# Conv attention with softmax over 256 keys: values of two row pairs in four column quarters, row sums from key tiles that GpSimd adds, and one turn of the context per eight rows

## Chip, cores and metric

One core of one Trainium2 chip runs the whole kernel as one launch. The metric is the device time of that core in microseconds; lower is better. The kernel before takes 2170.26 us, the median of 3 runs.

## The reference

A batch of 16 images with 128 channels and 32 x 32 pixels goes through three layers. The change touches the first alone:

```
g = group norm of x                                        # 32 groups of 4 channels
q = einsum('bchw,oc->bohw', g, qW)                         # 256 outputs: 8 heads x 32
k = einsum(..., BN(depthwise 3x3, stride 2, of g), kW)     # 32 x 256 keys
v = einsum(..., BN(depthwise 3x3, stride 2, of g), vW)     # 256 values x 32
attn = softmax(q.k / sqrt(4), over the 256 keys)           # q reshaped to rows of 32
ctx = attn @ v;   x = x + einsum('bchw,oc->bohw', ctx, oW)
```

Causal attention over each image's 1024 tokens and a mixture of 8 experts follow.

## The kernel before

The program has three blocks with a barrier between them: `conv_attention`, then `attention_and_routing`, then `expert_tiles`. Each engine's work is an instruction queue of its own, written out by hand, and semaphores are the only ties between them.

In `conv_attention` the work on an image is a period of eight turns, one for each pair (`i` from 0 to 7). A pair stands for four rows `h` of the queries, each with 256 columns of them, so 1024 softmax rows. `over_images` runs the periods as a loop over two images with the first and last written out. The stages of one pair are spread over several turns:

- `scores` (TensorE) makes plain scores of the pair `i + 3` in two banks `s_bank`, a row at a time; `row_max` (VectorE) reduces each to the negated maximum over keys.
- `turn_maxes` transposes the maxima of pair `i + 2` into `m_bank`; `max_high` (ScalarE) and `max_low` (VectorE) split them; SyncE's `shift_rows` sends them as two rows below the queries in `q_stack`.
- `shifted_scores` of pair `i` come out transposed, keys on partitions, in two banks `st_bank`, in two chunks `c` of 512 columns; `exps` (ScalarE) takes the exponential into `probsT`.
- `values` of pair `i - 1`: the stationary tile `v_ones` has 32 columns of values, one of ones for the row sums, and zeros up to 64. The two chunks go to the two column halves of the array and so to the two halves of the partitions of `o_bank`.
- `evacuate_context` (ScalarE) copies `o_bank` to `ctxT`; in the next turn `turn_context` transposes it into `c_bank`, and `normalise` (VectorE) takes the reciprocal of the sums there and multiplies.

Beside that run, for a coming image: `channel_stats`, `group_means`, `group_spread`, `group_variances`, `group_norm`, then `keys_values` (nine taps, each a matmul, whose stationary tile holds three copies of the key weights and one of the values' in 128 columns) and `queries` in four parts. `query_high`, `query_low` split each part, and SyncE (`queries_in`, eight transfers) and GpSimd (`queries_low_in`, four) lay it out in `q_stack`. `project` and `add_output` make the result of half an image. All of these use one bank, `front`.

What orders the work around the change is the text of each engine's `period`. On TensorE a turn reads so before, and this is the order that the times below belong to:

```
shifted_scores(b, slot, i, 0); turn_context(pair i - 2)
scores(pair i + 3, 0); scores(.., 1); turn_maxes(pair i + 2)
shifted_scores(b, slot, i, 1)
[group_variances at i == 0, group_means at i == 7]
values(pair i - 1)
scores(pair i + 3, 2); scores(.., 3)
[keys_values at 1; queries at 0, 2, 4, 6; project at 3 and 7]
```

## Time and profile before

| | us |
|---|---|
| median of 3 runs (2168.64 to 2171.3) | 2170.26 |
| the profiled execution, its own time | 2174.15 |
| its span, first to last instruction | 2172.4 |
| TensorE busy in the span | 1961.4 |
| VectorE busy | 1375.0 |
| ScalarE busy | 989.7 |
| GpSimd busy | 1029.3 |

The span is what the trace covers; the profiled execution's time has 1.75 us around it. Busy time is an average over three blocks that have different limits. The conv attention runs from the start to about 841 us; its last projection starts at 839.66 us and the next block's first scores at 842.84 us. In the rows, L733 are the shifted scores, L715 the scores, L745 the values, L753 the turned context, L723 the turned maxima, L635 the taps, L657 the queries, L678 the projection. A matmul of 32-bit floats with a plain (not the rounded, `F32R`) type shows as two records.

### The profile page before, as it was taken

The numbers are of one execution on the slowest core, as the hardware profiler recorded it, in microseconds if no ns is written. First come the engines' busy times: TensorE is split into PE (matmuls) and PEld (weight loads), VectorE is DVE, ScalarE is ACT, GpSimd is POOL, SyncE is SP. The second block draws the span as 40 slices with busy tenths as digits, with TensorE's granted clock in tenths as the row PEclk, the third lists the DMA queues.
The fourth block names the chain that finished last, engine by engine and source line by source line (L and its number), as shares of the span: only waits on it lengthen the run. The fifth ranks groups of instructions, "written<-read, shape, count | busy, mean of one in ns | idle before, by whom it ended". The sixth has DMA issues, their size and how long they took to land. (4 is left out here: it accounts for less than half of the span.)

```text
span 2172.4 us, 44335 instructions
## 1 busy us (share of the span) xinstructions
PE 1961.4 (90%) x11636; PEld 1466.1 (67%) x11636; DVE 1375.0 (63%) x3923; ACT 989.7 (46%) x2194; POOL 1029.3 (47%) x1367
## 2 busy tenths in 40 slices
PE   3999999999999998888898888887189999999997
PEld 2666666666666654665666666555189999999997
DVE  3676766767767665787788878876434444444443
ACT  0554555555455554444344333342045555555554
POOL 1221121212112111445554555555658888888887
PEclk9999999999999999999999999998589999999999
DMA  5322222222223222111111111111234444454454
GB/s 195 74 66 71 61 71 64 65 70 65 70 60 73 62 61 74 54 36 38 41 38 41 36 38 35 42 38 40 66 57 64 64 65 63 63 65 65 63 65 51
DMA packets 175423, 131.90 MB, mean 61 GB/s; under 512 B 33437, under 2 KB 164933, under 8 KB 175301
## 3 DMA queue, kind: packets, MB, share of 16 engines
q0 software_dynamic: 55808, 52.50, 15.1%
q1 hardware_dynamic: 118341, 77.16, 13.6%
q8 instruction: 86, 1.41, 0.3%
q10 hardware_dynamic: 1152, 0.54, 0.1%
q14 instruction: 36, 0.29, 0.0%
HBM read 31.47 MB, written 46.71 MB: 36 GB/s over the span
## 5 line engine op out<-in xcount | busy, mean ns | idle before, releaser
L1664 POOL DMA_INDIRECT out<-f_y,f_rows x272 | 424.1, 1559 | 45.5 <-POOL f_waited L1662 41.7
L447 DVE TENSOR_REDUCE neg_max<-s_bank 128x2 f32<-128x512 f32 x512 | 329.5, 685 | 133.5 <-PE s_bank L715 131.4
L1727 DVE SCALAR_TENSOR_TENSOR f_hidden<-f_silu,f_rows,f_h_bank 128x341 f32<-128x341 f32 x272 | 155.4, 571 | 307.6 <-ACT f_silu L1696 279.7
L567 ACT ACTIVATE probsT<-st_bank 128x512 f32<-128x512 f32 x512 | 276.6, 593 | 133.9 <-PE st_bank L733 133.6
L1096 POOL DMA_INDIRECT routed<-a_rows,a_target_idx x256 | 253.2, 989 | 68.6 <-issue 68.3
L335 POOL TENSOR_TENSOR waited<-nothing 128x1 int32<-128x1 int32 x64 | 12.1, 189 | 514.0 <-DVE q_low L436 514.0
L1473 PE MATMUL a_score_bank<-t_eT,t_gT 128*128 128x512 f32 x512 | 252.4, 617 | 1.2 <-DVE a_val L1140 1.2
L745 PE MATMUL o_bank<-probsT,v_ones 128*64 128x512 f32 x1024 | 248.0, 605 | 0.0
L1775 PE MATMUL f_y_bank<-w,f_hiddenT 114*128 (+1 forms) x1632 | 230.8, 277 | 1.3 <-ACT f_hiddenT L1688 1.3
L715 PEld LDWEIGHTS s_bank<-k_stack,q_stack 96*128 96x128 f32 x1024 | 141.9, 193 | 113.4 <-issue 94.0
L733 PE MATMUL st_bank<-q_stack,k_stack 98*128 98x512 f32 x512 | 214.0, 484 | 0.6 <-ACT probsT L567 0.5
L1775 PEld LDWEIGHTS f_y_bank<-w,f_hiddenT 114*128 114x128 f32 (+1 forms) x1632 | 203.1, 191 | 8.5 <-issue 1.8
L715 PE MATMUL s_bank<-k_stack,q_stack 96*128 96x256 f32 x1024 | 195.9, 312 | 6.9 <-DMA q_stack<-q_high 6.0
L1498 PE MATMUL a_sum_bank<-a_val,a_causal_probsT 128*128 128x129 f32 x1152 | 162.7, 289 | 41.1 <-DVE X L1204 36.9
L1688 ACT ACTIVATE f_hiddenT<-f_hT_bank 114x384 f32<-114x384 f32 x272 | 133.8, 492 | 144.2 <-issue 74.6
L1756 PE MATMUL f_h_bank<-w_high,f_xT_high 128*128 x544 | 196.3, 363 | 0.0
L1498 PEld LDWEIGHTS a_sum_bank<-a_val,a_causal_probsT 128*128 128x128 f32 x1152 | 147.7, 201 | 67.0 <-issue 61.0
L1696 ACT ACTIVATE f_silu<-f_h_bank 128x341 f32<-128x341 f32 x272 | 124.2, 457 | 124.1 <-PE f_h_bank L1759 122.3
L1185 DVE TENSOR_REDUCE a_row_neg_max<-a_score_bank 128x1 f32<-128x1024 f32 x128 | 155.8, 1217 | 37.3 <-PE a_score_bank L1473 19.7
L1106 POOL TENSOR_TENSOR a_causal_probs<-a_causal_probs,a_tril 128x128 f32<-128x128 f32 x128 | 58.5, 457 | 252.9 <-DVE a_causal_probs L1192 246.0
L1756 PE MATMUL f_h_bank<-w,f_xT_high 128*128 x544 | 173.1, 320 | 0.0
L1369 ACT ACTIVATE a_causal_probs<-a_score_bank,a_row_neg_max 128x128 f32<-128x128 f32 (+7 forms) x128 | 94.7, 740 | 141.0 <-DVE a_row_neg_max L1185 141.0
(210 smaller groups left out, 3591.7 us busy)
## 6 DMA issues: line engine op xcount, KB each, us to landing
q_stack<-q_high SPq DMA_DIRECT2D x512, 64.0 KB, 2.3
f_rows<-routed SPq DMA_DIRECT2D x272, 66.0 KB
q_stack<-q_low POOLq DMA_DIRECT2D x256, 64.0 KB, 2.6
out<-X SPq DMA_DIRECT2D x16, 512.0 KB, 3.2
X<-in_x SPq DMA_DIRECT2D x1, 6144.0 KB, 22.1
out<-f_y,f_rows POOLq DMA_INDIRECT x272
q_stack<-max_rows SPq DMA_DIRECT2D x256, 4.0 KB
routed<-a_rows,a_target_idx POOLq DMA_INDIRECT x256
```

The source lines that it names most:

```text
L447: dve.tensor_reduce(neg_max[:, i % 2, CT * j:CT * (j + 1)], s_bank[h % 2][:], AX_X, ALU.max, negate=True).then_inc(max_ready, 1)
L567: act.activation(probsT[:, i % 2, c, lt, :], st_bank[lt][:], ACT.Exp).then_inc(exp_done, 1)
L715: last = pe.matmul(s_bank[h % 2][:, t, :], q_stack[0:STACK, h, t * P:(t + 1) * P], k_stack[0:STACK, slot, :], start=(t == 0), stop=(t == C ...
L733: pe.matmul(st_bank[lt][:], k_stack[:, slot, lt * P:(lt + 1) * P], q_stack[:, h:h + 2, :].rearrange("p h c -> p (h c)"), start=True, stop= ...
L745: last = pe.matmul(o_bank[HALF * c:HALF * (c + 1), :], v_ones[:, slot, lt, :], probsT[:, i % 2, c, lt, :], start=(lt == 0), stop=(lt == LT ...
L1096: pool.indirect_dma_start(out=routed, out_offset=bass.IndirectOffsetOnAxis(ap=target_idx[:, slot, t, k:k + 1], axis=0), in_=rows[:, slot, ...
L1185: dve.tensor_reduce(neg_max[:, i % 2:i % 2 + 1], s_bank[i % 2][:], AX_X, ALU.max, negate=True).then_inc(max_ready, 1)
L1473: last = pe.matmul(s_bank[i % 2][:, 512 * h:512 * (h + 1)], gT[:, slot, i * P:(i + 1) * P], eT[:, slot, 512 * h:512 * (h + 1)], start=True ...
L1498: last = pe.matmul(o_bank[:], probsT[:, i % 2, t, :], val[:, slot, t, :], start=(t == 0), stop=(t == i))
L1664: pool.indirect_dma_start(out=out, out_offset=bass.IndirectOffsetOnAxis(ap=rows[:, i, TOKEN:TOKEN + 1].bitcast(I32), axis=0), in_=y[:, i, ...
L1756: pe.matmul(bank[:, 0:PADDED], xT_high[:, n % (2 * AHEAD), :], parts[part][:, of_expert], start=(part == 0), stop=False, skip_group_check= ...
L1775: last = pe.matmul(y_bank[:], hiddenT[0:m, n % 2, j, :], w2[0:m, bass.ds(e, 1), j, :], start=(j == 0), stop=(j == CHUNKS - 1))
```

## The change

Pairs are taken two by two, as octets of eight rows. `values` runs for an octet, in even turns, after `scores` of rows 2 and 3: the four chunks go to the four column quarters (`QUAD` = 32), with stationary tiles of 32 columns of values and no ones. The row sums come apart from that: GpSimd adds the two key tiles of each chunk (`add_keys`, into free halves of `tokens.eT` and `tokens.gT`) and four matmuls with the selector `ones_at` write the sums of octet `o` to row `o` of each quarter of a new bank, `sum_bank`. `m_bank` is given up for it: the turned maxima now go to the first quarter of `c_bank`. The context is turned once per octet, in odd turns, and ScalarE copies it unscaled to `raw` (`evacuate_turned`). The sums of an image are turned, inverted and applied in turns 2 and 3 of the next image (`turn_sums`, `invert_sums`, `scale`), and the two projections move to turns 3 and 5 there. The nine taps are split in five and four, with 64-column tiles in the two column halves; VectorE adds the halves (`keys_values`), and `split_keys` makes its copies from the one set of keys. `q_high` and `q_low` have two slots, and `probsT` has four.

```diff
+        v_rows = sb("v_rows", [P, 2, LT, KD])
+        ones_at = sb("ones_at", [P, OCTETS, QUAD])
+        q_high = sb("q_high", [P, Q_SLOTS, 2, CP], F32R)
+        q_low = sb("q_low", [P, Q_SLOTS, 2, CP], F32R)
...
-        probsT = sb("probsT", [P, 2, CHUNKS_PER_PAIR, LT, COLS])
+        probsT = sb("probsT", [P, 4, CHUNKS_PER_PAIR, LT, COLS])
         ctxT = sb("ctxT", [P, 2, COLS])
-        rsum = sb("rsum", [P, 2, 4, 2])
-        context = sb("context", [P, ROWS, CT, KD])
+        sumT = sb("sumT", [P, COLS])
+        rsum = sb("rsum", [P, ROWS * CT])
+        raw = sb("raw", [P, ROWS * CT, KD])
+        context = sb("context", [P, ROWS * CT, KD])
...
-        m_bank = ps("m_bank", [P, P])
+        sum_bank = ps("sum_bank", [P, COLS])
+        m_bank = c_bank[:, 0, :]
+        def key_sum(cc):
+            return (tokens.eT, tokens.gT)[cc // 2][:, 1, COLS * (cc % 2):COLS * (cc % 2 + 1)]
...
+                def add_keys(b, i):
+                    if i % 2 == 0:
+                        wait(pool, o_full, octet_no(b, i // 2))
+                    for c in range(CHUNKS_PER_PAIR):
+                        pool.wait_ge(exp_done, PAIR_EXPS * pair_no(b, i) + LT * (c + 1))
+                        pool.tensor_tensor(key_sum(CHUNKS_PER_PAIR * (i % 2) + c), probsT[:, i % 4, c, 0, :],
+                                           probsT[:, i % 4, c, 1, :], ALU.add).then_inc(key_sums, 1)
...
                 def keys_values(b, slot):
                     dve.wait_ge(kv_full, b + 1)
-                    dve.tensor_scalar(kv[:, slot, :], front[:, 0:L], kv_bias[:], None, ALU.add).then_inc(kv_ready, 1)
+                    dve.tensor_scalar(kv[:, slot, :], front[KV:2 * KV, 0:L], kv_bias[:], None, ALU.add
+                                      ).then_inc(kv_half, 1)
+                    dve.wait_ge(kv_half, b + 1)
+                    dve.tensor_tensor(kv[:, slot, :], kv[:, slot, :], front[0:KV, 0:L], ALU.add).then_inc(kv_ready, 1)
...
-                def normalise(b, slot, i):
...
-                                      .to_broadcast([P, 2, 4, KD]), ALU.mult).then_inc(ctx_done, 1)
...
+                def invert_sums(b):
+                    dve.wait_ge(sums_turned, b + 1)
+                    dve.reciprocal(rsum[:].rearrange("p (j c n) -> p j c n", j=OCTETS, c=OCTET_CHUNKS),
+                                   c_bank[:].rearrange("p n (c j) -> p j c n", j=QUAD)[:, 0:OCTETS]
+                                   ).then_inc(rsum_ready, 1)
+                    dve.wait_ge(rsum_ready, b + 1)
+                def scale(b, k):
+                    dve.wait_ge(c_out, OCTETS * (b + 1))
+                    wait(dve, out_full, 2 * (b - 1) + k + 1)
+                    part = slice(ROWS * k, ROWS * (k + 1))
+                    dve.tensor_tensor(context[:, part, :], raw[:, part, :],
+                                      rsum[:, part].unsqueeze(2).to_broadcast([P, ROWS, KD]), ALU.mult
+                                      ).then_inc(scaled, 1)
...
-                        turned = pair(b, slot, i - 2)
-                        if has(turned[0]):
-                            normalise(*turned)
+                        if i == 2 and has(b - 1):
+                            invert_sums(b - 1)
                         turning = pair(b, slot, i + LEAD - 1)
                         if has(turning[0]):
                             max_low(*turning)
+                        if i == 2 and has(b - 1):
+                            scale(b - 1, 0)
...
+                            scale(b - 1, 1)
+                            add_output(b - 1, 0)
...
+                def evacuate_context(b, slot, o):
+                    act.wait_ge(o_full, octet_no(b, o) + 1)
+                    wait(act, c_full, octet_no(b, o) - 1)
+                    act.activation(ctxT[:, o % 2, :], o_bank[:], ACT.Copy).then_inc(ctxT_full, 1)
+                    if o == OCTETS - 1:
+                        act.activation(sumT[:], sum_bank[:], ACT.Copy).then_inc(sums_out, 1)
+                def evacuate_turned(b, slot, o):
+                    act.wait_ge(c_full, octet_no(b, o) + 1)
+                    wait(act, scaled, 2 * b - (o < OCTETS // 2))
+                    rows = slice(2 * PAIR_ROWS * CT * o, 2 * PAIR_ROWS * CT * (o + 1))
+                    act.activation(raw[:, rows, :].rearrange("p (c n) d -> p n c d", c=OCTET_CHUNKS),
+                                   c_bank[:].rearrange("p n (c d) -> p n c d", d=KD), ACT.Copy).then_inc(c_out, 1)
...
+                    halves = ((4, 0, 1, 2, 7), (5, 3, 6, 8))
+                    for n in range(len(halves[0])):
+                        for part, taps in enumerate(halves):
+                            if n == len(taps):
+                                continue
+                            t = taps[n]
+                            di, dj = divmod(t, 3)
+                            out = front[KV * part:KV * (part + 1), 0:L].rearrange("p (i j) -> p i j", j=SIDE // 2)
+                            last = pe.matmul(out[:, di == 0:, dj == 0:], tap_w[:, t, :],
+                                             xn[:, (1, 0, 1)[di]:SIDE - (di == 0):2, (1, 0, 1)[dj]:SIDE - (dj == 0):2],
+                                             start=(n == 0), stop=(n == len(taps) - 1), skip_group_check=True)
...
-                def values(b, slot, i):
-                    if i == 0:
+                def values(b, slot, o):
+                    if o == 0:
                         pe.wait_ge(v_in, 16 * LT * (b + 1))
-                    pe.wait_ge(exp_done, PAIR_EXPS * (pair_no(b, i) + 1))
-                    wait(pe, ctxT_full, pair_no(b, i))
+                        wait(pe, sums_out, b)
+                    pe.wait_ge(key_sums, OCTET_CHUNKS * (octet_no(b, o) + 1))
+                    wait(pe, ctxT_full, octet_no(b, o))
                     for lt in range(LT):
-                        for c in range(CHUNKS_PER_PAIR):
-                            last = pe.matmul(o_bank[HALF * c:HALF * (c + 1), :], v_ones[:, slot, lt, :],
-                                             probsT[:, i % 2, c, lt, :], start=(lt == 0), stop=(lt == LT - 1))
+                        for cc in range(OCTET_CHUNKS):
+                            i, c = divmod(cc, CHUNKS_PER_PAIR)
+                            pe.matmul(o_bank[QUAD * cc:QUAD * (cc + 1), :], v_rows[:, slot, lt, :],
+                                      probsT[:, (2 * o + i) % 4, c, lt, :], start=(lt == 0), stop=(lt == LT - 1))
+                    for cc in range(OCTET_CHUNKS):
+                        last = pe.matmul(sum_bank[QUAD * cc:QUAD * (cc + 1), :], ones_at[:, o, :], key_sum(cc),
+                                         start=(o == 0), stop=(o == OCTETS - 1), skip_group_check=True)
                     last.then_inc(o_full, 1)
-                def turn_context(b, slot, i):
-                    pe.wait_ge(ctxT_full, pair_no(b, i) + 1)
-                    wait(pe, ctx_done, pair_no(b, i))
+                def c_bank_free(b, i):
+                    turning = pair(b, 0, i + LEAD - 1)
+                    wait(pe, m_low_done, pair_no(turning[0], turning[2]) if has(turning[0]) else PAIRS * NB)
+                def turn_context(b, slot, o):
+                    pe.wait_ge(ctxT_full, octet_no(b, o) + 1)
+                    wait(pe, c_out, octet_no(b, o))
+                    wait(pe, rsum_ready, b)
                     for n in range(4):
-                        last = pe.transpose(c_bank[:, n, :], ctxT[:, i % 2, n * P:(n + 1) * P], ident[:])
+                        last = pe.transpose(c_bank[:, n, :], ctxT[:, o % 2, n * P:(n + 1) * P], ident[:])
                     last.then_inc(c_full, 1)
+                def turn_sums(b):
+                    pe.wait_ge(sums_out, b + 1)
+                    pe.wait_ge(c_out, OCTETS * (b + 1))
+                    for n in range(4):
+                        last = pe.transpose(c_bank[:, n, :], sumT[:, n * P:(n + 1) * P], ident[:])
+                    last.then_inc(sums_turned, 1)
...
+                        summed = octet(b, slot, i)
+                        turned = i % 2 and has(summed[0])
+                        if turned:
+                            c_bank_free(b, i)
+                            turn_context(*summed)
+                        if i == 2 and has(b - 1):
+                            c_bank_free(b, i)
+                            turn_sums(b - 1)
                         if has(scored[0]):
                             scores(*scored, 0)
                             scores(*scored, 1)
                         if has(turning[0]):
+                            if turned:
+                                pe.wait_ge(c_out, octet_no(summed[0], summed[2]) + 1)
+                            if i == 2:
+                                wait(pe, rsum_ready, b)
                             turn_maxes(*turning)
                         if has(b):
                             shifted_scores(b, slot, i, 1)
@@ -773,12 +847,11 @@
                             group_variances(new)
                         if i == PAIRS - 1 and has(b + 2):
                             group_means(b + 2)
-                        summed = pair(b, slot, i - 1)
-                        if has(summed[0]):
-                            values(*summed)
                         if has(scored[0]):
                             scores(*scored, 2)
                             scores(*scored, 3)
+                        if i % 2 == 0 and has(summed[0]):
+                            values(*summed)
...
                         if i == 3 and has(b - 1):
+                            project(b - 1, 0)
+                        if i == 5 and has(b - 1):
                             project(b - 1, 1)
-                        if i == PAIRS - 1 and has(b):
```

TensorE in two neighbouring turns. Before, one turn from turning the context to scores of rows 2 and 3; `x3` are repeats:

```order
L753 MATMUL c_bank<-ident,ctxT 128x128 [waits ctx_done,ctxT_full]
L753 MATMUL c_bank<-ident,ctxT 128x128 x3
L715 MATMUL s_bank<-k_stack,q_stack 128x256 [waits max_ready]
L715 MATMUL s_bank<-k_stack,q_stack 128x256
L715 MATMUL s_bank<-k_stack,q_stack 128x256 [waits max_ready]
L715 MATMUL s_bank<-k_stack,q_stack 128x256
L723 MATMUL m_bank<-ident,neg_max 128x128 [waits m_low_done,max_ready]
L733 MATMUL st_bank<-q_stack,k_stack 128x512 [waits exp_done] x2
L745 MATMUL o_bank<-probsT,v_ones 64x512 [waits ctxT_full,exp_done]
L745 MATMUL o_bank<-probsT,v_ones 64x512 x3
L715 MATMUL s_bank<-k_stack,q_stack 128x256 [waits max_ready]
L715 MATMUL s_bank<-k_stack,q_stack 128x256
```

In the changed kernel an odd turn, from turning the context of an octet:

```order
L811 MATMUL c_bank<-ident,ctxT 128x128 [waits c_out,rsum_ready,ctxT_full,m_low_done]
L811 MATMUL c_bank<-ident,ctxT 128x128 x3
L761 MATMUL s_bank<-k_stack,q_stack 128x256 [waits q_low_in0,max_ready,q_in0,k_ready]
L761 MATMUL s_bank<-k_stack,q_stack 128x256
L761 MATMUL s_bank<-k_stack,q_stack 128x256 [waits max_ready]
L761 MATMUL s_bank<-k_stack,q_stack 128x256
L769 MATMUL c_bank<-ident,neg_max 128x128 [waits m_low_done,max_ready,c_out]
L779 MATMUL st_bank<-q_stack,k_stack 128x512 [waits exp_done] x2
L761 MATMUL s_bank<-k_stack,q_stack 128x256 [waits max_ready]
L761 MATMUL s_bank<-k_stack,q_stack 128x256
L761 MATMUL s_bank<-k_stack,q_stack 128x256 [waits max_ready]
L761 MATMUL s_bank<-k_stack,q_stack 128x256
```

and the end of the even turn before it, from the scores of row 3 to the queries:

```order
L761 MATMUL s_bank<-k_stack,q_stack 128x256 [waits max_ready]
L761 MATMUL s_bank<-k_stack,q_stack 128x256
L793 MATMUL o_bank<-probsT,v_rows 32x512 [waits ctxT_full,key_sums]
L793 MATMUL o_bank<-probsT,v_rows 32x512 x7
L796 MATMUL sum_bank<-t_eT,ones_at 32x512 x2
L796 MATMUL sum_bank<-t_gT,ones_at 32x512 x2
L709 MATMUL front<-qwT,xn 128x256 [waits out_done,q_low_done]
L709 MATMUL front<-qwT,xn 128x256
```

The values no longer stand between the two pairs of scores, and the turned maxima of an odd turn wait for `c_out`, which `evacuate_turned` raises.

ScalarE in the changed kernel, an odd turn and the even one after it: L609 are the exponentials, L623 is the copy of the turned context, L602 the maxima, L614 the copy of `o_bank`, L595 the queries:

```order
L609 ACTIVATE probsT<-st_bank 128x512 [waits st_full,o_full]
L609 ACTIVATE probsT<-st_bank 128x512 [waits st_full]
L623 ACTIVATE raw<-c_bank 128x4x4x32 [waits scaled,c_full]
L602 ACTIVATE max_rows<-c_bank 8x128 [waits m_in1,m_full]
L609 ACTIVATE probsT<-st_bank 128x512 [waits st_full] x2
L609 ACTIVATE probsT<-st_bank 128x512 [waits st_full,o_full]
L609 ACTIVATE probsT<-st_bank 128x512 [waits st_full]
L602 ACTIVATE max_rows<-c_bank 8x128 [waits m_in0,m_full]
L609 ACTIVATE probsT<-st_bank 128x512 [waits st_full] x2
L614 ACTIVATE ctxT<-o_bank 128x512 [waits c_full,o_full]
L595 ACTIVATE q_high<-front 128x512 [waits q_in3,q_full]
```

Before, the odd turn had no instruction between its exponentials and the maxima, and `ctxT` was copied in every turn:

```order
L567 ACTIVATE probsT<-st_bank 128x512 [waits st_full,o_full]
L567 ACTIVATE probsT<-st_bank 128x512 [waits st_full]
L560 ACTIVATE max_rows<-m_bank 8x128 [waits m_in1,m_full]
L567 ACTIVATE probsT<-st_bank 128x512 [waits st_full] x2
L572 ACTIVATE ctxT<-o_bank 128x512 [waits c_full,o_full]
```

VectorE in turns 1 and 2, where keys and values arrive. Before:

```order
L422 TENSOR_SCALAR kv<-front,kv_bias 128x256 [waits kv_full]
L426 CAST k_stack<-kv 64x256 [waits kv_ready]
L427 CAST k_high<-kv 32x256
L429 TENSOR_TENSOR k_stack<-kv,k_high 32x256 [waits k_high_ready]
L447 TENSOR_REDUCE neg_max<-s_bank 128x2 [waits m_full,s_full]
L447 TENSOR_REDUCE neg_max<-s_bank 128x2 [waits s_full]
L465 RECIPROCAL rsum<-c_bank 128x2x4 [waits c_full,out_done]
```

and in the changed kernel:

```order
L459 TENSOR_SCALAR kv<-front,kv_bias 64x256 [waits kv_full]
L462 TENSOR_TENSOR kv<-kv,front 64x256 [waits kv_half]
L466 CAST k_stack<-kv 32x256 [waits kv_ready]
L467 CAST k_stack<-kv 32x256
L469 TENSOR_TENSOR k_stack<-kv,k_stack 32x256 [waits k_high_ready]
L487 TENSOR_REDUCE neg_max<-s_bank 128x2 [waits m_full,s_full]
L487 TENSOR_REDUCE neg_max<-s_bank 128x2 [waits s_full]
L500 RECIPROCAL rsum<-c_bank 128x64 [waits sums_turned]
L493 TENSOR_TENSOR max_rows<-c_bank,max_rows 8x128 [waits m_high_done,rsum_ready]
```

There is one more operation before the keys are split, and between the row maxima and `max_low` stands a reciprocal of 64 elements, for whose end the turned maxima wait.

## Rows read from the trace of the kernel before

**Rows 1.** The page: the span, and busy time, share and instructions by engine.
```profile
span 2172.4 us, 44335 instructions
...
PE 1961.4 (90%) x11636; PEld 1466.1 (67%) x11636; DVE 1375.0 (63%) x3923; ACT 989.7 (46%) x2194; POOL 1029.3 (47%) x1367
```

**Rows 2.** One image by windows: length, busy of PE, PEld, DVE, ACT, POOL; clock.
```profile
401.20:450.30 49.10, 48.37 (x247) 30.14 (x246) 34.25 (x75) 25.29 (x53) 10.12 (x21) 1.00 0.27 66
```

**Rows 3.** Timeline of TensorE: the shifted scores that open turns 1 to 0, and 1.
```profile
404.55 0.81 PE L733 MATMUL st_bank<-q_stack,k_stack 98*128 98x512 f32 x2
...
413.09 0.82 PE L733 MATMUL st_bank<-q_stack,k_stack 98*128 98x512 f32 x2
...
418.44 0.83 PE L733 MATMUL st_bank<-q_stack,k_stack 98*128 98x512 f32 x2
...
424.74 1.02 PE L733 MATMUL st_bank<-q_stack,k_stack 98*128 98x512 f32 x2
...
430.31 0.82 PE L733 MATMUL st_bank<-q_stack,k_stack 98*128 98x512 f32 x2
...
435.20 0.64 PE L733 MATMUL st_bank<-q_stack,k_stack 98*128 98x512 f32 x2
...
440.66 0.82 PE L733 MATMUL st_bank<-q_stack,k_stack 98*128 98x512 f32 x2
...
447.97 1.03 PE L733 MATMUL st_bank<-q_stack,k_stack 98*128 98x512 f32 x2
...
453.66 0.82 PE L733 MATMUL st_bank<-q_stack,k_stack 98*128 98x512 f32 x2
```

**Rows 4.** Timeline of turn 5: start, length, engine, line, operation, count.
```profile
430.70 0.60 ACT L553 ACTIVATE q_high<-front 128x512 fp32r<-128x512 f32 x1 [0.93 <-PE front L657]
...
430.97 0.60 PE L753 MATMUL c_bank<-ident,ctxT 128*128 128x128 f32 x4
431.19 1.08 ACT L567 ACTIVATE probsT<-st_bank 128x512 f32<-128x512 f32 x2
...
431.88 0.27 PE L723 MATMUL m_bank<-ident,neg_max 128*128 128x128 f32 x1
...
431.91 0.91 PE L733 MATMUL st_bank<-q_stack,k_stack 98*128 98x512 f32 x2
...
432.75 1.94 PE L745 MATMUL o_bank<-probsT,v_ones 128*64 128x512 f32 x8
...
434.62 0.74 PE L715 MATMUL s_bank<-k_stack,q_stack 96*128 96x256 f32 x4
```

**Rows 5.** Timeline of TensorE at the first records of a group of values.
```profile
432.75 0.65 PE L745 MATMUL o_bank<-probsT,v_ones 128*64 128x512 f32 x2
```

**Rows 6.** Timeline of TensorE: taps, a projection, a part of the queries.
```profile
409.44 4.01 PE L635 MATMUL front<-xn,tap_w 128*128 128x256 f32 x18
...
423.42 1.88 PE L678 MATMUL front<-context,owT 128*128 128x512 f32 x4
...
429.63 1.03 PE L657 MATMUL front<-qwT,xn 128*128 128x256 f32 x4
```

**Rows 7.** Timeline of VectorE in turn 7.
```profile
443.81 1.29 DVE L447 TENSOR_REDUCE neg_max<-s_bank 128x2 f32<-128x512 f32 x2
```

**Rows 8.** Timeline of VectorE after the taps: keys, then the first row maxima.
```profile
413.48 0.48 DVE L422 TENSOR_SCALAR kv<-front,kv_bias 128x256 f32<-128x256 f32 x1 [2.80 <-PE front L635]
...
415.06 1.29 DVE L447 TENSOR_REDUCE neg_max<-s_bank 128x2 f32<-128x512 f32 x2
```

**Rows 9.** GpSimd's groups by form: busy, mean ns of one, idle before.
```profile
L337 POOL DMA_DIRECT2D q_stack<-q_low x256 | 143.7, 567 | 2.9 <-issue 2.9
...
L1106 POOL TENSOR_TENSOR a_causal_probs<-a_causal_probs,a_tril 128x128 f32<-128x128 f32 x128 | 58.5, 457 | 252.9 <-DVE a_causal_probs L1192 246.0 <-issue 6.2
...
L1091 POOL TENSOR_TENSOR w<-w,w_high 128x341 fp32r<-128x341 f32 x16 | 14.2, 910 | 6.1 <-ACT w_high L1390 6.1
```

**Rows 10.** VectorE's output sum, 300 to 600 us, by form.
```profile
L476 DVE TENSOR_TENSOR X<-X,front 128x512 f32 x13 | 8.9, 688 | 9.8 <-PE front L678 9.8
```

155 lines of the change are left out of this document (66 added, 89 removed).

## The prediction

> **What bounds the kernel now.** I read the page first [rows 1]: TensorE is busy for 90% of the span, but over three stages with different limits, and the change touches only the first, the conv attention of 16 images. The view by windows and the timeline of the shifted-score matmuls, which open every turn of the loop over row pairs, give that stage's rhythm [rows 2, 3]. The reader is to see eight turns per image, of 4.9 to 8.5 us, 49.1 us together, 16 times; in them TensorE 48.4 us busy, VectorE 34.3, ScalarE 25.3, GpSimd 10.1. So TensorE's queue sets the pace. But its busy time holds waits: in turn 5 [rows 4] the second pair of shifted scores takes 0.91 us where the same pair in turn 6 takes 0.64 at 435.20, pipeline included [rows 3], because its bank waits for an exponential. What the array must stream is, for a turn, 0.86 for two shifted pairs, 0.44 to turn the context (four records in 0.60, 0.17 of it pipeline [rows 4]), 0.96 for four rows of scores, 0.11 for the maxima and 1.97 for the values with their way in and out: 4.34, times 8 = 34.7; with queries 3.4, two projections 3.5, taps 3.65 and the group sums 0.6 it comes to 45.9 us an image. The other 3.2 us are waits.
>
> **What the change takes off TensorE.** (1) Values. Eight matmuls stand in 1.87 us (432.75 to 434.62): four steps of 0.43 us, in each two records that overlap, 0.65 us for both [rows 5], plus 0.15 for getting in and out. That they overlap in pairs is the evidence that column parts run side by side. Afterwards a group has 16 value and 8 row-sum matmuls; side by side by four that is 6 steps, 6 x 0.43 + 0.15 = 2.73 us per two pairs. 8 x 1.87 becomes 4 x 2.73: 4.0 us less an image. Bounds: two by two it is 12 steps, 5.3 us a group; four by four is the least. I take four, since the two-part form shows no loss. The Trainium skill, TensorE: Matmul & The Clock Gate, section Part 3: Packing small matmuls, measured 2.38 times for three column parts, not 3; by that ratio the estimate for a group would be 3.4 us and the result 43 us higher. No run here shows three or four. (2) Taps: 18 matmuls in 3.65 us (409.44 to 413.09) [rows 3, 6] become 10 steps of 0.2 plus 0.15 = 2.2: 1.4 less. (3) Turning: four transposes take 0.43 us; 8 groups become 4 and one for the sums: 1.3 less. Sum: 6.8 us of stream an image, 109 us over 16. If TensorE's stream were all, this would be a large gain.
>
> **What the change adds on the path.** It moves the values behind the scores of rows 2 and 3, so they no longer cover the row maxima; it puts the transposed maxima into the bank of the turned context; and it hangs work on GpSimd. I walk the turns, from the moment the array starts a turn (0.19 us after the stamp where a long matmul precedes it).
>
> *Odd turns.* In turn 5 [rows 4] ScalarE does q_high at 430.70, then two exponentials, 431.19 to 432.27, one per 0.49 us. The new copy of the turned bank is queued behind them: 432.18 to 432.78. Only then may the maxima be transposed, at 432.93; it was 431.88. Then second shifted scores 0.43 and scores 0.5 us: 433.9, 3.4 us after the start, where the stream alone is 2.4. With the projection (1.75: four steps of 0.43 and the way in) [rows 6] turns 3 and 5 take 5.2 us each. Queued behind that transpose on TensorE are the second half of the turn's exponentials and row maxima, so all engines slide.
>
> *Even turns.* The shifted pair ends at 1.9 (exponentials); row_max of rows 0 and 1 (1.29 us a pair) ends at 2.2 to 2.4, so row 3's scores end at 2.6 to 2.8 instead of 1.5. Then values 2.8 and queries 0.9 [rows 6]: 6.5 for turn 4 (VectorE still has the output sum in front), 6.3 for turn 6.
>
> *Turn 7.* Statistics hold VectorE: row_max of row 0 starts 3.15 us after the stamp (440.66 to 443.81) [rows 3, 7]. Before, the values stood there and covered most of it. Now the scores of rows 2 and 3 come at once and wait for the two reductions, and row 3's end at 4.7. *Turn 0* starts with rows 2 and 3 of turn 7 not yet reduced (group_spread stands before them): its first scores wait 1.1 to 1.6 us: 7.0. *Turn 1*: group_norm is ready at 4.1, the taps run 4.2 to 6.4 and leave: 6.6.
>
> *Turn 2.* Keys to first row_max took 1.58 us, 413.48 to 415.06 [rows 8]. The second kv operation adds 0.46 (such an operation takes 0.48, overlapping the next by a little): 2.05. Two row_max 1.29, then the reciprocal of the 64 sums (no row has it: more than nothing, less than the 0.69 of 512 elements [rows 10]; I take 0.26, near the small end), then the transposed maxima, which wait for rsum_ready: 3.7, not 1.4. Scores end at 4.7, values 7.5, queries 8.4; it was 5.35.
>
> Sum: 5.2 + 6.5 + 5.2 + 6.3 + 4.7 + 7.0 + 6.6 + 8.4 = 49.9 us against 49.1. The same arithmetic over the old turns gives 48.7, so it runs 0.4 short: 50.3.
>
> *GpSimd.* No row shows a 128x512 add. 128x128 took 457 ns and 128x341 910 ns [rows 9]: 2.13 ns an element, 1.27 us at 512. Lower bound: that line; upper: 457 ns x 4 = 1.83. I take 1.27, since 341 is the nearer row. From one group of values to the next, the tightest case (turn 4 to 6) leaves 8.7 us: two adds 2.55, then waiting for q_low and four DMA issues of 0.567 us, to about 5.0, then two adds: 7.6. It fits by 1.1 us and costs nothing; at 1.83 it is 1.1 us late.
>
> *Shared reads.* VectorE's scale reads raw and rsum, 1024 elements; 512 took 0.69 [rows 10], so 1.2 to 1.4. In turn 3 it falls where GpSimd adds. Its price is between nothing (both run at once) and 1.27 us (it waits for one add), passed on through the output sum to turn 4: I take 0.4 an image. The Trainium skill, SBUF — State Buffer, says that a VectorE instruction with two SBUF inputs and a GpSimd instruction that reads SBUF lock each other out whole; no row here shows it. By that rule it is 0.9 in turn 4, by its absence 0.
>
> So 50.7 us an image: +1.6, x 16 = +26 us. **The tail**: after the last image there was one projection; now values 2.8, two copies 1.3, two turns 1.0, reciprocal 0.3, scale 1.3, projection and output sum 2.6 and the second pair of these 2.3, 11.6, stand against values 2.0, copy 0.7, turn 0.4, normalise 0.6, projection and sum 2.6, 6.3: +5. Other stages have the same code: 0. **Sum**: profiled time 2174.2 + 31 = 2205; the median of the runs lies 3.9 lower than the profiled execution: 2201.
>
> **The rivals.**
> A, forecast: waits eat the gain, 2201; own range 2185 to 2228. Chance 0.56.
> B, faster: TensorE's queue fills what I call waits. What decides is the copy of the turned bank and the late row_max: if they add under 6.5 us an image, it wins. With the waits of before, 3.2 us, on 39.1 us of stream an image takes 42.3 us: 2174 - 109 + 5 - 4 = 2066; between that and my 10.8 us of waits lie 2066 and 2201; half way is 2134. For: TensorE is named at 98% busy in the stage. Against: [rows 4, 7] show the places where it already waits. Chance 0.22.
> C, the four column parts do not run four wide: two by two adds 6 steps, 2.6 us a group, 10.3 an image: 2201 + 165 = 2366. For: nothing shows four. Against: two show no loss. Chance 0.07. That would be the change not doing what it says.
> D, GpSimd sets the pace: at 1.83 us an add the values wait 1.1 us a group, 4.4 an image, 70 in all: 2271. For: 457 ns for 128 elements and the DMA issues between the adds. Against: 128x341. Chance 0.10.
> Cancelling out within 0.2%: 0.05.
>
> **How the numbers follow.** A is likeliest: 2201. The range must reach into B's upper part and to D's lower: 2140 to 2245 leaves 0.13 below and 0.11 above at most. 0.2% (4.3 us) is about what a measurement of this kernel can tell from no change. Slower: A, C, D, 0.73; faster 0.22; same 0.05.
>
> **What would show it.** In the new profile: a group of values of 2.7 us with records in fours (C: 5.3); taps 2.2 us; in odd turns TensorE's transposed maxima ended by ScalarE's copy of c_bank, about 1 us late; in turn 2 by VectorE's reciprocal; TensorE's wait for key_sums near nothing (D: about 1 us a group); the add at 1.27 us; an image period 50.7 us, with about 39 us of stream. An add far above 1.3 us, or a period under 49 us with those waits short, would make the forecast wrong. So would a late q_stack transfer, since SyncE issues shift_rows behind eight q_high transfers, which I cost at nothing: two turns lie between.

## The result, and the profile after

The changed kernel takes 2343.24 us (median of 4 runs, 2339.63 to 2350.25) against 2170.78 us: ratio 1.0799, 95% interval 1.0769 to 1.0829. It is slower, as forecast, but by 172 us instead of 31. All of it is in the conv attention: from the next block's first scores to the end it is 1329.8 us, 1329.6 before. ScalarE does 32 exponentials an image there; by the groups of instructions between 300 and 800 us it now does 264 where it did 328, which is 60.6 us an image after 48.8 (49.1 in [rows 2]). The forecast was 50.7. The first image, which has none before it, is not slower (46.8 us after 47.4), so the whole is less than 16 times the difference.

The page of the changed kernel, in its first rows and the row of TensorE's clock, one digit for each fortieth of the span:

```profile
span 2337.9 us, 45281 instructions
...
PE 1978.3 (85%) x11956; PEld 1451.1 (62%) x11956; DVE 1400.3 (60%) x3732; ACT 997.2 (43%) x2210; POOL 1347.9 (58%) x1623
...
PEclk8897989899888988999999999999859999999999
```

TensorE's busy time has grown by 17 us [rows 1] although 109 us of stream went out of it. The clock row says why to look further: 8 and 9 stand over the conv attention. The windows of one image, turn by turn from turn 5 on (length, busy of PE, PEld, DVE, ACT, POOL, then the granted clock), to be held against [rows 2, 3]:

```profile
507.40:512.50 5.10, 4.14 (x22) 3.03 (x21) 3.47 (x6) 3.42 (x7) 5.08 (x8) 1.00 0.40 90
512.50:519.10 6.60, 6.60 (x43) 3.42 (x42) 3.31 (x6) 2.87 (x6) 2.15 (x3) 1.00 0.21 52
519.10:524.40 5.30, 3.79 (x22) 2.73 (x20) 3.98 (x9) 3.42 (x7) 5.28 (x8) 1.00 0.40 92
524.40:535.30 10.90, 9.19 (x42) 5.01 (x43) 5.84 (x10) 2.96 (x7) 2.49 (x4) 0.69 0.11 29
535.30:543.80 8.50, 6.97 (x38) 4.71 (x36) 4.17 (x7) 3.92 (x9) 7.16 (x9) 0.80 0.39 93
543.80:552.70 8.90, 6.42 (x47) 3.77 (x46) 6.24 (x12) 2.98 (x6) 0.54 (x1) 1.00 0.03 5
552.70:557.80 5.10, 4.14 (x23) 2.98 (x22) 3.50 (x7) 3.42 (x7) 5.08 (x8) 1.00 0.40 97
557.80:566.30 8.50, 6.93 (x44) 3.43 (x42) 5.90 (x7) 2.87 (x6) 2.14 (x3) 1.00 0.14 36
```

Turns 5, 6, 7, 0, 1, 2, 3, 4 take 5.1, 6.6, 5.3, 10.9, 8.5, 8.9, 5.1 and 8.5 us; the forecast was 5.2, 6.3, 4.7, 7.0, 6.6, 8.4, 5.2 and 6.5. In turns 0 and 1 the clock reads 0.69 and 0.80 of 2.4 GHz, so part of each ran at the 1.2 GHz level; before, it reads 1.00 [rows 2]. Of the 12 inner images, the third to the fourteenth, turn 0 is low in all (a reading below 0.9), turn 1 in seven, turn 2 in eight and turn 4 in six: the same turn, with the same waits, is low in one image and not in the next.

Timeline of TensorE, the same groups at full and at low clock, and the waits of turns 7, 0 and 2 (in brackets, with what ended them):

```profile
515.62 1.92 PE L793 MATMUL o_bank<-probsT,v_rows 128*32 128x512 f32 x16
...
518.34 1.13 PE L709 MATMUL front<-qwT,xn 128*128 128x256 f32 x4
...
521.89 0.30 PE L769 MATMUL c_bank<-ident,neg_max 128*128 128x128 f32 x1 [1.04 <-ACT raw L623]
...
526.81 1.39 PE L761 MATMUL s_bank<-k_stack,q_stack 96*128 96x256 f32 x4 [1.71 <-DVE neg_max L487]
...
530.48 3.28 PE L793 MATMUL o_bank<-probsT,v_rows 128*32 128x512 f32 x16
...
539.90 3.96 PE L688 MATMUL front<-xn,tap_w 128*64 128x256 f32 x18 [0.48 <-DVE xn L454]
...
547.92 0.30 PE L769 MATMUL c_bank<-ident,neg_max 128*128 128x128 f32 x1 [2.48 <-DVE rsum L500]
```

A group of values and sums takes 518.34 - 515.62 = 2.72 us in turn 6, as forecast; in turn 0 the same 16 value records take 3.28 instead of 1.92. The taps take 3.96, not 2.2. And behind these waits stands VectorE, whose timeline shows two operations far over their time:

```profile
524.01 1.89 DVE L442 TENSOR_TENSOR dmean<-mv,gmean 128x1 f32<-128x1 f32 x1
525.94 0.22 DVE L444 SCALAR_TENSOR_TENSOR spread<-dmean,mv 128x1 f32<-128x1 f32 x1
...
548.86 1.20 DVE L509 TENSOR_TENSOR context<-raw,rsum 128x1024 f32<-128x1024 f32 x1
...
557.67 2.85 DVE L509 TENSOR_TENSOR context<-raw,rsum 128x1024 f32<-128x1024 f32 x1
```

GpSimd's timeline beside it:

```profile
523.37 2.50 POOL L372 TENSOR_TENSOR t_gT<-probsT 128x512 f32<-128x512 f32 x2
...
556.92 2.52 POOL L372 TENSOR_TENSOR t_gT<-probsT 128x512 f32<-128x512 f32 x2
```

A subtraction of one element per partition ends at 525.90, with the second of GpSimd's two additions (525.87). The scale of turn 3 ends 1.1 us after the additions do, having waited for both; that of turn 2, with no addition near, takes 1.20.

So three theories went into the experiments. **W**: waits in TensorE's queue, as forecast. **L**: GpSimd's additions and some VectorE operations lock each other out. **C**: TensorE's granted clock falls where it now stands still for longer.

### The profile page after: what moved, and what is told of

It is laid out like the page before. It is cut to its first block and busy times, and to the rows that moved or that the text cites. A ratio compares the mean times of both kernels' runs of the same rounds, so it can differ in the third digit from the quotient of the medians.

```text
span 2337.9 us, 45281 instructions
## 1 busy us (share of the span) xinstructions
PE 1978.3 (85%) x11956; PEld 1451.1 (62%) x11956; DVE 1400.3 (60%) x3732; ACT 997.2 (43%) x2210; POOL 1347.9 (58%) x1623
## 5 line engine op out<-in xcount | busy, mean ns | idle before, releaser
L372 POOL TENSOR_TENSOR t_eT<-probsT 128x512 f32<-128x512 f32 x128 | 161.1, 1279 | 395.6 <-PE sum_bank L796 395.6
L609 ACT ACTIVATE probsT<-st_bank 128x512 f32<-128x512 f32 x512 | 277.6, 595 | 129.8 <-PE st_bank L779 126.3
L761 PE MATMUL s_bank<-k_stack,q_stack 96*128 96x256 f32 x1024 | 214.2, 329 | 60.3 <-DVE neg_max L487 50.7
L761 PEld LDWEIGHTS s_bank<-k_stack,q_stack 96*128 96x128 f32 x1024 | 170.5, 213 | 97.5 <-DVE neg_max L487 78.3
L779 PE MATMUL st_bank<-q_stack,k_stack 98*128 98x512 f32 x512 | 222.3, 507 | 1.4 <-ACT probsT L609 0.8
L476 DVE TENSOR_TENSOR q_low<-front,q_high 128x512 fp32r<-128x512 f32 x64 | 44.3, 692 | 256.9 <-ACT q_high L595 256.9
L793 PE MATMUL o_bank<-probsT,v_rows 128*32 128x512 f32 x1024 | 165.2, 776 | 2.0 <-POOL t_gT L372 1.9
```

The costliest lines, as they stand in the source:

```text
L372: pool.tensor_tensor(key_sum(CHUNKS_PER_PAIR * (i % 2) + c), probsT[:, i % 4, c, 0, :], probsT[:, i % 4, c, 1, :], ALU.add).then_inc(key_s ...
L609: act.activation(probsT[:, i % 4, c, lt, :], st_bank[lt][:], ACT.Exp).then_inc(exp_done, 1)
L761: last = pe.matmul(s_bank[h % 2][:, t, :], q_stack[0:STACK, h, t * P:(t + 1) * P], k_stack[0:STACK, slot, :], start=(t == 0), stop=(t == C ...
L779: pe.matmul(st_bank[lt][:], k_stack[:, slot, lt * P:(lt + 1) * P], q_stack[:, h:h + 2, :].rearrange("p h c -> p (h c)"), start=True, stop= ...
L793: pe.matmul(o_bank[QUAD * cc:QUAD * (cc + 1), :], v_rows[:, slot, lt, :], probsT[:, (2 * o + i) % 4, c, lt, :], start=(lt == 0), stop=(lt ...
```

## The experiments

Ratios are to the kernel before on the same chip, with 95% intervals. W, L and C are named in the expectations as above.

### 1 and 2: one operand from PSUM; the second scale a turn later

```
- dve.tensor_tensor(dmean[:], mv[:, 0:1], gmean[:], ALU.subtract)
+ dve.tensor_tensor(dmean[:], mv[:, 0:1], front[:, 0:1], ALU.subtract)
```
and for the second, besides:
```
  if i == 3 and has(b - 1):
-     scale(b - 1, 1)
      add_output(b - 1, 0)
+ if i == 4 and has(b - 1):
+     scale(b - 1, 1)
```

> Edit: VectorE's subtraction for the group means takes its second operand from the PSUM bank front instead of the SBUF copy gmean, so that it has one SBUF input; nothing else changes. In the changed kernel this operation on 128x1 takes 1.89 us where it took 0.16 us before, and it stands in VectorE's queue ahead of the last two row maxima of turn 7, which open turn 0. Theory L (GpSimd's additions and VectorE operations with two SBUF inputs lock each other out): it falls back to about 0.2 us, turn 0 becomes 1.7 us shorter, 27 us over 16 images, 2316 us; if TensorE's granted clock also recovers in turns 0 and 1, up to 2290. Theory W (only the in-order waits of TensorE): the operation keeps 1.9 us or is not on the path, and the time stays within 5 us of 2343. Theory C (the granted clock is most of the loss): the period goes down by more than the 1.7 us that the operation gives back only if the clock of turns 0 and 1 rises from 0.69 and 0.80.

> Edit: as the first (the mean from PSUM), and the second scale of the context (1024 elements, two SBUF inputs) stands in turn 4 of VectorE instead of turn 3, away from GpSimd's additions of turn 3; the output sum stays where it was, in turn 3. In the changed kernel this scale takes 2.85 us where that of turn 2 takes 1.20. Theory L: it falls to 1.2 us if no addition runs beside it, and turn 4 becomes up to 1.6 us shorter than with the first edit, 16 to 26 us over 16 images; it stays near 2.8 if GpSimd's additions of turn 4 meet it there. Theory W: the place of the scale changes the time by under 10 us. Theory C: a further gain beyond 26 us goes with a higher granted clock in turns 4 to 6.

Measured: 1.0779 [1.0761, 1.0797] and 1.0647 [1.0629, 1.0664]. VectorE's timeline of the first:

```profile
523.66 0.15 DVE L442 TENSOR_TENSOR dmean<-mv,front 128x1 f32<-128x1 f32 x1
523.85 1.70 DVE L444 SCALAR_TENSOR_TENSOR spread<-dmean,mv 128x1 f32<-128x1 f32 x1
```

The lock did not go away, it went to the next operation with two SBUF inputs, so nothing clear of noise was gained, where the expectation had 27 us. In the second, the scale's mean fell to 1.34 us (between 300 and 900 us; 2.10 before the edit). Turn 4 takes 6.6 us in every inner image, where it took 8.5 at full clock and up to 11.5, and turn 5 takes 6.0 instead of 5.2, since the moved scale makes its output sum late. The second is 29 us below the first, a little more than L's 16 to 26.

### 3: matmuls of zeros where TensorE waits

```
+ def fill(b, times, wait_out=True):
+     ...
+     for n in range(times):
+         pe.matmul(sum_bank[:], zeros[:], ..., start=False, stop=False, skip_group_check=True)
```

> Edit: the changed kernel with matmuls of zeros that add nothing to the bank of the row sums, put where TensorE waits: one of 128x512 ahead of the wait for the turned bank in turns 1, 3, 5 and 7, two ahead of the wait for the reciprocal in turn 2, two at the start of turn 0, one in turn 4. It is 9 of 0.43 us, 3.9 us of stream an image, of which an estimate of 1 us lies outside the waits. Theory C (TensorE's granted clock falls in turns 0, 1 and 4 since TensorE stands still for longer there): the granted clock of the stage goes from about 0.86 towards 1.00, and the time falls by 40 to 110 us. Theories W and L (the waits and the locked operations by themselves): the clock does not matter, the time is the same or rises by 16 to 60 us.

Measured: 1.0422 [1.0404, 1.0439], 82 us less than the changed kernel's ratio, with nothing taken away and 7.7 us an image of useless stream added: nine matmuls are 18 records of 0.43 us, and the expectation had counted one for each. Windows of turns 0, 1, 2 and 4:

```profile
486.00:494.40 8.40, 8.27 (x48) 4.29 (x48) 5.80 (x10) 2.90 (x7) 2.60 (x4) 1.00 0.16 39
494.40:501.30 6.90, 6.25 (x40) 4.16 (x38) 4.18 (x7) 3.87 (x9) 6.88 (x9) 1.00 0.43 105
501.30:510.10 8.80, 8.04 (x49) 4.29 (x49) 6.25 (x12) 2.98 (x6) 0.70 (x2) 1.00 0.07 13
...
515.30:523.80 8.50, 7.79 (x46) 3.75 (x44) 5.88 (x7) 2.87 (x6) 2.13 (x3) 1.00 0.14 36
```

Turns 0 and 1 fall from 10.9 and 8.5 to 8.4 and 6.9. Turns 2 and 4 keep the 8.9 and 8.5 that they have at full clock: there the zeros lie inside the waits and cost nothing. The granted clock reads 1.00. C is shown. In turn 0 the zeros cost nothing either, since they end when the row maximum is there:

```profile
486.60 1.88 PE L822 MATMUL sum_bank<-tap_w,zeros 128*128 128x512 f32 x4
488.47 1.10 PE L763 MATMUL s_bank<-k_stack,q_stack 96*128 96x256 f32 x4
...
487.73 2.67 DVE L489 TENSOR_REDUCE neg_max<-s_bank 128x2 f32<-128x512 f32 x4
```

The scores start 0.74 us after VectorE starts the reduction, as in the changed kernel (526.07 and 526.81). So the image of 3, 54.5 us (486.04 to 540.53), is that of the changed kernel at full clock. Eleven of the 12 inner images are like it; in one, turn 4 is low and the image takes 58.8.

### 13 and 14: the zeros in turns 7 and 0 alone, and in turn 2 alone

```
# 13                                        # 14
  if turned:                                  if i == 2:
+     if i == PAIRS - 1: fill(b, 1)         +     fill(b, 2)
      pe.wait_ge(c_out, ...)                      wait(pe, rsum_ready, b)
+ if i == 0: fill(b, 2, False)
```

> Edit: the changed kernel with matmuls of zeros in two turns only: one of 128x512 in turn 7 ahead of the wait for the turned bank and two at the start of turn 0; 1.3 us of stream an image instead of 3.9. If the waits of turns 7 and 0 take the clock down in turns 0 and 1, these two turns read 1.00 and the kernel gains 50 to 75 us of the 82 that all the fills gave: ratio 1.045 to 1.057. Turns 2 and 4, which read below 1.00 in about every second image, keep that if their cause is turn 2. Rival: every wait counts alike, and a third of the fill gives a third of the gain: ratio 1.065 to 1.072.

> Edit: the changed kernel with two matmuls of zeros in turn 2 only, ahead of the wait for the reciprocal. If turn 2's wait is the cause of the low clock in turns 2 and 4, these two read 1.00 and the image becomes 1.5 to 2.5 us shorter, 25 to 40 us over 16: ratio 1.061 to 1.069; turns 0 and 1 stay at 0.69 and 0.80. If turns 7 and 0 are the cause of all, the ratio stays within 0.004 of 1.080.

Measured: 1.0625 [1.058, 1.0671] and 1.0668 [1.0631, 1.0704]. Windows of 13, turns 2, 4 and 0:

```profile
469.90:481.50 11.60, 9.11 (x45) 4.70 (x45) 6.24 (x12) 3.03 (x6) 0.45 (x1) 0.71 0.03 4
486.70:498.20 11.50, 8.60 (x43) 3.65 (x42) 7.21 (x7) 2.87 (x6) 3.42 (x4) 0.85 0.16 38
515.20:523.60 8.40, 8.29 (x48) 4.31 (x48) 5.79 (x10) 2.92 (x7) 2.60 (x4) 1.00 0.16 40
```

and of 14, turns 2 and 4, then turn 0 of the next image:

```profile
468.30:477.20 8.90, 8.14 (x51) 4.36 (x50) 6.24 (x12) 2.99 (x6) 0.83 (x2) 1.00 0.07 13
482.40:494.50 12.10, 9.29 (x42) 4.08 (x41) 7.27 (x7) 2.86 (x6) 3.33 (x4) 0.72 0.15 35
511.50:522.50 11.00, 9.79 (x44) 5.25 (x43) 5.92 (x10) 2.94 (x7) 2.55 (x4) 0.59 0.13 31
```

Each fill repairs its own turns. In 13 turn 0 takes 8.5 us at clock 1.00 in every inner image, but turn 2 is now low in ten of the 12 and turn 4 in seven; 14 frees turn 2, and turn 0 stays low in all 12 and turn 4 in ten. So there is no single wait to blame: turn 2 falls when turn 0 doesn't, turns 0 and 4 when turn 2 doesn't. What decides in which images a turn is low is not shown. 13 gave 38 us of the 50 to 75 that its expectation had. 14 gave 29, within its range, but by more in turn 2 and nothing in turn 4: its expectation named turn 2 as the cause for turn 4 as well; that was wrong.

### 4: no additions on GpSimd

```
- if has(b): add_keys(b, i)
- pe.matmul(sum_bank[...], ones_at[:, o, :], key_sum(cc), ...)
+ for lt in range(LT):
+     pe.matmul(sum_bank[...], ones_at[:, o, :], probsT[:, (2 * o + i) % 4, c, lt, :], ...)
```

> Edit: GpSimd adds nothing; the selector matmuls run on the exponentials themselves, twice as many of them, 2 steps of 0.43 us more in each group of values. Stream: 0.86 us x 4 an image more, 55 us over 16. Theory L: the subtraction of the means falls to 0.2 us, the scale of turn 3 to 1.2 us, which give back 1.7 and 1.6 us an image, 53 us: the time stays about 2343, within 20. With theory C beside it (shorter waits and more stream hold the granted clock up): 2240 to 2300. Theory W: the waits stay and the stream is added, 2360 to 2400.

Measured: 1.077 [1.0752, 1.0788]. The subtraction is back at 0.16 us and every scale at 1.21, yet the clock between 300 and 900 us reads 0.90 (0.88 with the additions). TensorE's waits in that stretch:

```profile
PE c_bank L767 <- ACT raw L621: 39.5, 40, 1.1
PE c_bank L767 <- DVE rsum L498: 24.8, 10, 2.5
```

They are the same as in the changed kernel, 4 x 1.0 and 2.5 us an image, and turns 0, 1 and 2 are still low in 12, five and seven of the 12 images: no lock is needed for the clock to fall. The time came out as L said: what the locks gave back went into the 55 us of added stream.

### 6 and 7: no shared reads left; with zeros too

```
- dve.tensor_tensor(dmean[:], mv[:, 0:1], front[:, 0:1], ALU.subtract)
+ dve.tensor_tensor(front[:, 2:3], mv[:, 0:1], front[:, 0:1], ALU.subtract)
- dve.scalar_tensor_tensor(out=spread[:], in0=dmean[:], scalar=dmean[:], in1=mv[:, 1:2], ...)
+ dve.scalar_tensor_tensor(out=spread[:], in0=front[:, 2:3], scalar=front[:, 2:3], in1=mv[:, 1:2], ...)
```

> Edit: as the one with the later scale (ratio 1.065), and the difference of the means is kept in a free PSUM column, so that the next operation, the spread, has one SBUF input as well. In the first experiment the lock had only moved: the subtraction fell from 1.89 to 0.16 us and the spread behind it rose from 0.22 to 1.70. Theory L: now both are 0.2, turn 0 becomes 1.5 us shorter, 24 us over 16 images: ratio about 1.054; with more granted clock down to 1.045. Rival: GpSimd holds something else that VectorE needs, the next instruction takes the 1.7 us, and the ratio stays at 1.065.

> Edit: the sixth kernel (no locked operation on 128x1, the scale later) with the matmuls of zeros of the third, which bring the granted clock of the stage to 1.00 at 54.9 us an image. If the locked operations and the clock together are all that the prediction left out, the image takes what its walk of the turns gave and the fill's part outside the waits: 54.9 - 1.7 (the two on 128x1) - 1.5 to 2.2 (the scale) = 51.0 to 51.7 us, ratio 1.013 to 1.020. Rival: the walk itself was short by 2 us or more an image, the ratio stays above 1.03.

Measured: 1.0494 [1.0467, 1.0521] and 1.0382 [1.0361, 1.0403]. In 6 both operations on 128x1 take their 0.16 and 0.22 us, while the additions are still there: it was the second SBUF input. The ratio lies between the two that L gave, with and without more clock, and an image takes 55.8 us, 4.8 less than in the changed kernel. Windows of 7, turns 0, 1, 2, 3, 4, 5, 6 and 7:

```profile
530.60:538.50 7.90, 7.81 (x49) 4.22 (x48) 4.23 (x10) 2.95 (x7) 2.84 (x4) 1.00 0.20 49
538.50:545.10 6.60, 6.12 (x39) 4.07 (x37) 4.08 (x7) 3.81 (x8) 6.58 (x9) 1.00 0.46 109
545.10:554.00 8.90, 8.14 (x50) 4.37 (x50) 6.24 (x12) 2.99 (x6) 0.85 (x2) 1.00 0.07 13
554.00:559.20 5.20, 5.10 (x26) 3.31 (x24) 3.46 (x6) 3.42 (x7) 5.18 (x8) 1.00 0.40 97
559.20:566.40 7.20, 7.20 (x45) 3.71 (x44) 3.36 (x6) 2.87 (x6) 2.09 (x3) 1.00 0.16 42
566.40:572.40 6.00, 5.58 (x24) 3.26 (x23) 4.67 (x7) 3.42 (x7) 5.98 (x8) 1.00 0.37 90
572.40:579.00 6.60, 6.60 (x43) 3.42 (x42) 3.32 (x6) 2.87 (x6) 2.30 (x3) 1.00 0.14 40
579.00:584.10 5.10, 4.55 (x23) 2.94 (x21) 3.77 (x9) 3.42 (x7) 5.08 (x8) 1.00 0.36 85
```

Apart from what the edits add, this is the forecast's kernel: full clock, no lock. Its image takes 53.7 us (530.62 to 584.33; the last window stops 0.2 us short). Of it, 0.8 are zeros in turn 0 (an estimate: its scores start at 532.40 where the row maximum, begun at 530.85, would let them start at 531.6); about 0.6 are zeros in turn 4 (6.6 in 6), and 0.9 lie in turn 5, where the output sum now comes late because the scale was moved. Without them it is 51.4, against 49.9 by the walk. These costs of the edits, 2.3 us an image or about 0.017 of the ratio, are why 7 missed its range (1.013 to 1.020); the walk was short by 1.5 us, not by the rival's 2. So at full clock the locks are worth 54.5 - 51.4 = 3.1 us an image, 1.9 in turn 4 and 1.2 in turn 0, some 45 us in all. Between the changed kernel and 6, where the moved scale costs 0.9 us in turn 5, an image gains 4.8, 66 us in all: the larger part is the locks' own time, the rest came through the clock.

### 5 and 8: the values ahead of the scores again

```
+ if i % 2 == 0 and has(summed[0]): values(*summed)
  scores(*scored, 2); scores(*scored, 3)
- if i % 2 == 0 and has(summed[0]): values(*summed)
```
In 8 the four row-sum matmuls stay behind, the locks are out as in 6, and ScalarE copies the turned bank between its first two exponentials.

> Edit: the changed kernel with the group of values and row sums ahead of the scores of rows 2 and 3 in TensorE's queue, where the values stood before, instead of behind them. Theory W (a row maximum is no longer covered by the values): even turns lose 0.5 to 1.2 us each where TensorE waited for neg_max, 2 to 4 us an image, 32 to 64 us: ratio 1.05 to 1.065, if the sums of GpSimd are ready by then. Rival: the group now waits for key_sums instead, since GpSimd's last addition ends some 2.5 us after the last exponential of the odd turn; the time stays within 10 us or rises, ratio 1.075 to 1.10. Theory C: any gain is larger than the waits removed, as the clock rises.

> Edit: the sixth kernel with, further, the 8 value matmuls ahead of the scores of rows 2 and 3 (they wait for the exponentials only) and the 4 row-sum matmuls behind them, and in the odd turns ScalarE's copy of the turned bank between the first two exponentials instead of behind them. Theory W: the row maxima are covered again, 2 to 4 us an image, and the maxima are turned 0.4 us earlier in four turns, 1.6 us: 3.6 to 5.6 us an image less than the sixth, ratio 1.01 to 1.03 by the waits alone, and 0.99 to 1.01 if the clock comes back to 1.00 with them. Rival: other waits (the output sum, the statistics in turn 7) take their place and the ratio stays above 1.04.

Measured: 1.0516 [1.0484, 1.0549] and 1.0463 [1.0442, 1.0483]. 5 gains as W said: turns 4 and 6 take 6.4 us each (8.5 at full clock and 6.6 before the edit), and turn 4 is never low. An image is 3.9 us shorter, 2.3 of it at equal clock; the wait for GpSimd's sums is 1.8 us in 600. 8 misses, and its rival holds: the copy's wait halved (21.0 us in 44 times, longest 0.6) and turn 3 lost 0.5 us, but turn 5 stays at 6.0, the clock at 0.92, and turn 2 with its wait for the reciprocal (26.3 us in 11 times) is untouched. The normalisation also grew, from a mean of 0.80 us to 1.28.

### 9 and 10: the taps alone; all but the taps

9 is the kernel before with `halves = ((4, 0, 1, 2, 7), (5, 3, 6, 8))`, the second operation on kv, and the narrower kv_w, tap_w and kv. 10 is the changed kernel with `halves = ((4, 0, 1, 2, 7, 5, 3, 6, 8),)` and one operation on kv.

> Edit: the kernel before with the taps in two column halves and the two operations on kv, and nothing else of the change. By the prediction's own terms: 1.45 us less of TensorE's stream an image, and 0.46 us more on VectorE between taps and row maxima: 1.0 us an image less, 16 us over 16, ratio 0.993. Theory W: the row maxima of turn 2 start 0.5 us later and eat part of it, ratio 0.995 to 1.000. Theory C: the stage is at clock 1.00 and TensorE is 98% busy, so that 1.45 us less work does not bring the clock down; if it does in turn 1 or 2, the ratio is above 1.00.

> Edit: the changed kernel with that one part undone: nine taps into one column part, one operation on kv. At a given clock it adds 1.45 us of stream an image and takes 0.46 off VectorE: plus 1.0 us, 16 over 16 images, ratio 1.087. Theory C: more work in turn 1 makes the low clock of turns 1 and 2 rarer, so that part of it or more comes back: ratio 1.07 to 1.083. Without that theory 1.085 to 1.09.

Measured: 0.9899 [0.9881, 0.9917] and 1.0894 [1.0876, 1.0912]. TensorE's timeline of 9 around the taps:

```profile
494.50 2.34 PE L640 MATMUL front<-xn,tap_w 128*64 128x256 f32 x18
496.78 0.73 PE L738 MATMUL st_bank<-q_stack,k_stack 98*128 98x512 f32 x2
```

2.28 us where 3.65 stood [rows 6], with the clock at 1.00: turn 1 loses 1.3 us, no other turn changes by 0.1, and an image takes 47.8 us instead of 49.15, 22 us in all. VectorE's extra 0.46 us is hidden. 9 beats both kernels. The clock of 10 is that of the changed kernel (0.921 and 0.920), so the shorter taps did not bring it down; turns 1 and 2 are low in eleven and all of the 12 inner images, not more rarely as C had it.

### 11 and 12: two parts of the change on the kernel before

11 moves `values(*summed)` behind `scores(*scored, 3)` in every turn. 12 adds, at the places of add_keys:
```
+ pool.tensor_tensor(unused[:, 2 * (i % 2) + c, :], flat[:, 0:COLS], flat[:, COLS:2 * COLS], ALU.add)
```

> Edit: the kernel before with the values behind the scores of rows 2 and 3 in every turn, and nothing else of the change. Theory W: in eight turns the scores now wait for a row maximum that the values covered; by the walk of the prediction 0.3 to 1 us a turn, 2 to 6 us an image: ratio 1.015 to 1.045 at full clock. Theory C: if these waits alone take the clock down, it is above that, and the granted clock of the stage reads below 0.97. Rival: other waits shrink by as much, ratio below 1.01.

> Edit: the kernel before with 16 additions of 128x512 an image on GpSimd, at the places where the changed kernel has them, between operands that are of no use to anything, into a tile that nobody reads. TensorE and all waits stay as they are. Theory L: the operations on 128x1 (0.16 and 0.22 us) and the subtraction of the keys (0.42) become up to 1.3 to 1.7 us longer where they meet an addition; with the slack of VectorE in turn 7 that costs 0 to 2 us an image, ratio 1.000 to 1.015. Rival: GpSimd's own queue is late (the transfers of q_low, the inverse root for the norm), and the ratio goes above 1.015. At ratio 1.000 the additions by themselves cost nothing and only their meeting with the new scale does.

Measured: 1.0396 [1.038, 1.0412] and 1.0101 [1.0085, 1.0118]. TensorE in a turn of 11:

```profile
501.09 1.10 PE L715 MATMUL s_bank<-k_stack,q_stack 96*128 96x256 f32 x4
502.12 0.65 PE L745 MATMUL o_bank<-probsT,v_ones 128*64 128x512 f32 x2
```

The scores of rows 2 and 3 take 1.03 us instead of 0.58 (434.62 to 435.20 in [rows 3, 4]), because each row waits for a row maximum that the values used to cover; every turn is 0.4 to 1.1 us longer, at clock 0.99 (only turn 7 is low, in three images). This part of the change, alone and in all eight turns, costs 86 us. 12 costs 22 us, and not where expected. VectorE, GpSimd and TensorE in turn 1:

```profile
517.23 2.36 DVE L429 TENSOR_SCALAR xn<-X,gmean,grs 128x1024 f32 x1
...
517.74 1.29 POOL L348 TENSOR_TENSOR unused<-tap_w 128x512 f32<-128x512 f32 x1
...
519.64 0.71 PE L647 MATMUL front<-xn,tap_w 128*128 128x256 f32 x2 [0.95 <-DVE xn L429]
```

The normalisation, which has one SBUF tensor input and took 0.79 us, takes 2.36, and the taps wait for it: turn 1 is 1.3 us longer (9.8 after 8.6) and no other turn changes. It stood behind the last of GpSimd's DMA issues (to 517.72) and the first addition, and ended ahead of the second, which took 1.74 us. The subtraction and the spread grew to means of 0.27 and 1.04, but turn 7's values cover them.

## Why the prediction was wrong

**Right.** Four parts side by side ran with no loss: 2.72 us a group, against 2.73. The addition took 1.28 against 1.27, and TensorE hardly waited for key_sums, so rival D is out and C's two-wide with it. The Trainium skill, TensorE: Matmul & The Clock Gate, Part 3: Packing small matmuls, has 2.38 times for three column parts; four gave here what four would by the step count. The turned maxima of odd turns waited for ScalarE's copy 0.96 to 1.05 us, those of turn 2 for the reciprocal. Turn 1 took 6.6 us in 7, and turns 3 and 5 take 5.1 here, against 6.6, 5.2 and 5.2. The tail was right as well: from the start of the last exponential to the next block's first scores it is 17.6 us, 12.9 before, though part of it at a low clock (16.1 in 3). The direction was right, and for the reason given: by 7 the waits alone make an image 51.4 us where it was 49.15, and 11 shows one of them by itself.

**The step that failed: "So 50.7 us an image".** Every duration in that sum was read in a stage where TensorE is 98% busy and the clock 1.00 [rows 2], and none was priced for another clock. The changed kernel has TensorE busy for 3.79 of 5.30 us in turn 7, then standing 1.71 us in one wait. Its windows of 2 us from there on:

```profile
524.00:526.00 2.00, 1.01 (x4) 0.38 (x3) 1.95 (x2) 1.08 (x2) 1.88 (x2) 1.00 0.63 165
526.00:528.00 2.00, 1.19 (x4) 1.09 (x5) 1.61 (x4) 0.00 (x0) 0.00 (x0) 0.61 0.17 37
528.00:530.00 2.00, 2.00 (x9) 1.81 (x9) 1.38 (x4) 1.35 (x3) 0.24 (x1) 0.50 0.00 0
```

The clock goes from 1.00 to 0.50, the 1.2 GHz level, in the middle of that wait, and the work behind it pays. By 3, the image is 54.5 us at full clock; it is 60.6: 6.1 us an image is the clock, and 3 gave 82 of the 172 us back. The Trainium skill, TensorE: Matmul & The Clock Gate, section HAM oscillation — how this bites in real kernels, describes a kernel whose TensorE waits for a transfer before every tile and pays the low clock after each wait. The trace agrees that the fall comes with a wait, and differs in that it does not follow each: the wait of 2.48 us in turn 2 of this image leaves the clock at 1.00.

**Terms mis-sized.** *Shared reads*, 0.4 us an image with 1.27 as the upper end, "it waits for one add": they cost 3.1. An operation that meets two additions in a row waited for both. At full clock turn 4 takes 8.5 with the lock and, in 6, 6.6 without: 1.9. The Trainium skill, SBUF — State Buffer, section Who interferes with whom, states the lock, and I weighed it for the scale only; dmean, a subtraction of the same kind, stood ahead of the row maxima that open turn 0 (8.4 in 3, and 8.0 in 7, 0.8 of it zeros: 1.2). *The walk*: turns 2, 7 and 6 were short by 0.5, 0.4 and 0.3, turns 0, 1 and 4 by 0.1 or 0.2, so the walk was 1.5 short in all, of which the forecast had added 0.4. In turn 2, 0.3 of it is *the reciprocal*: 0.26 assumed, 0.55 measured. 49.9 + 1.5 + 1.9 + 1.2 = 54.5, which is the image of 3, and with 6.1 for the clock 60.6. Against the forecast's 50.7 the clock is 6.1 of the 9.9 us that were missing, the locks 2.7 and the walk 1.1.

**The rivals.** None named the clock. The range reached 2245 for D's sake. "My 10.8 us of waits" leaves out the two terms of 0.4; with 2201 go 11.6. What I gave as a gain of 6.8 us of stream left, where waits stood, a TensorE with less to do in them: 7.7 us of useless stream in these waits bring the clock back (3), 3.4 us outside them hardly do (4, 0.90 after 0.88), and with waits of at most 0.7 us and all the stream it stays at 0.99 (11). Whether the stream taken out or the new waits for `c_out` and `rsum_ready` weigh more was not tested, nor what each single wait costs.

## What to carry to other kernels

Where TensorE is nearly always busy, work taken off it is worth its time only if the waits beside it don't grow; the granted clock of the present kernel says nothing of the forecast one, so ask of each turn how long TensorE will stand in it, and price the waits twice, once in themselves and once for the stretch behind them at the lower level. Before GpSimd gets a long operation on SBUF, list every VectorE operation that reads two SBUF operands or copies SBUF to SBUF, the tiny ones first, since one of 128x1 can hold a queue for two additions. And split a change: of this one, the taps by themselves give 1.0%.

## What the runs showed of the hardware

- Useless matmuls of zeros inside waits, 7.7 us an image, made the kernel 3.5% faster (1.0422 against 1.0799), the granted clock going from 0.88 to 0.99 between 300 and 900 us.
- A VectorE operation with two SBUF inputs waited through two back-to-back additions: 1.89 us for 0.16 of work, 2.85 for 1.20. The normalisation of 12 got in between two of them, and the second took 1.74 us for 1.27. Taking away one operand moves the lock to the next operation (1.70 for 0.22).
- A `tensor_scalar` of 128x1024 from SBUF to SBUF is held up too: 2.36 us for 0.79 in 12, and in 8 still 1.24 beside GpSimd's DMA issues, with no addition running (497.57 to 498.81; the next addition starts at 498.93). The Trainium skill, SBUF — State Buffer, section Who interferes with whom, says that this form can take the shared pair; the trace agrees.
